# Filler matmuls between the waits of TensorE in a four-network graph kernel

## The reference

```
# GIN, 3 layers                                 # GATv2, 3 layers, 4/4/1 heads
edge_emb = edge_attr @ W + b                    m = xl[src] + xr[dst] + edge_attr @ We
msg  = relu(h_in[src] + edge_emb)               s = sum(leaky(m) * att)          per head
agg  = segment_sum(msg, dst)                    ex = exp(s - segment_max(s)[dst])
z    = two dense layers of (h_in + agg)         out = segment_sum(xl[src] * ex) / segment_sum(ex)
```

## Time and profile before

| | us |
|---|---|
| median of 3 runs | 11196.97 (11195.04 to 11202.61) |
| the profiled execution, own time | 11203.72 |
| its span, first to last instruction | 11201.9 |
| TensorE, busy | 7487.5 |
| VectorE, busy | 5111.4 |
| POOL, busy | 4643.1 |
| ScalarE, busy | 3374.1 |

### The profile page before, as it was taken

How to read it: one execution, slowest core, us unless ns; L and a number is a source line. 1 busy time by engine, 2 the same in 40 slices (tenths; PEclk the granted TensorE clock), 3 DMA queues, 4 the chain that set the end, 5 groups by cost and what they waited for, 6 DMA issues and landing times.

```text
span 11201.9 us, 174392 instructions
## 1 busy us (share of the span) xinstructions
PE 7487.5 (67%) x43333; PEld 4918.1 (44%) x43334; DVE 5111.4 (46%) x14634; ACT 3374.1 (30%) x10389; POOL 4643.1 (41%) x5386
## 2 busy tenths in 40 slices
PE   5999999567765666556665566665656665666665
PEld 2444598344443333333333444444444443444443
DVE  5888731211111111111115556666555666555667
ACT  1001220111120111111114445555444555444444
POOL 0000000566546666466554444443444443444442
PEclk9999999778877778777787777777777777777777
DMA  1001285222221111111112222221222221222221
GB/s 36 18 35 47 118 333 183 63 69 72 69 65 48 49 47 48 44 49 47 46 42 55 58 58 58 58 57 52 59 57 57 58 58 53 59 58 60 58 59 49
DMA packets 501741, 731.50 MB, mean 65 GB/s; under 512 B 128746, under 2 KB 406593, under 8 KB 485012
## 3 DMA queue, kind: packets, MB, share of 16 engines
q1 hardware_dynamic: 350484, 414.14, 11.2%
q0 software_dynamic: 150528, 308.58, 10.5%
HBM read 597.78 MB, written 124.32 MB: 64 GB/s over the span
## 4 chain that ended last, share of the span: by engine, by line
PE 24%; issue 18%; another core or an unknown queue 14%; DVE 13%; DVEq 2%; ACT 0%; DMA 0%; SPq 0%; POOL 0%; ACTq 0%; POOLq 0%
PE ps L806 5%; PE ps L982 4%; PE ps L918 4%; PE ps L910 4%; PE ps L985 3%; DVE ps L1428 2%; PE ps L993 2%; PE ps L1019 1%; DVE hr L1465 1%; DVE w L1417 1%; DVE w L1433 1%; DVE scanned L1423 1%; DVE sval L1410 1%; DVE mdif L1404 1%
## 5 line engine op out<-in xcount | busy, mean ns | idle before, releaser
L543 POOL DMA_INDIRECT rows_and_onehots<-node_table,idx x4704 | 4511.3, 959 | 2494.0 <-issue 1368.2
L806 PE MATMUL ps<-rows_and_onehots,w 128*128 128x128 f32 x5280 | 921.6, 330 | 1374.6 <-issue 1318.5
L538 POOL COPY idx<-src_g 128x8 int32 (+1 forms) x594 | 114.0, 192 | 3902.4 <-DMA node_table<-hr 2327.6
L806 PEld LDWEIGHTS ps<-rows_and_onehots,w 128*128 128x128 f32 x5280 | 830.1, 235 | 1880.7 <-issue 1768.6
L1290 DVE TENSOR_TENSOR agg<-agg,ps 128x128 f32 x660 | 189.5, 287 | 3027.3 <-remote 2036.4
L678 ACT ACTIVATE w<-ps 128x512 f32<-128x512 f32 x663 | 395.8, 597 | 3308.1 <-remote 1983.2
L1019 PE MATMUL ps<-ident,scanned 20*128 20x20 f32 (+1 forms) x1332 | 328.9, 322 | 1352.5 <-DVE scanned L1423 982.2
L1417 DVE TENSOR_TENSOR w<-rows_and_onehots,ps 128x512 f32<-128x512 f32 x669 | 458.7, 686 | 1644.9 <-remote 1451.2
L982 PE MATMUL ps<-w_L_gnn_We,hr 128*128 128x512 f32 x1344 | 1078.6, 896 | 97.8 <-issue 45.1
L985 PEld LDWEIGHTS ps<-xrb,w 128*128 128x128 bf16 x8064 | 704.2, 123 | 606.0 <-issue 606.0
L993 PE MATMUL ps<-hr,rows_and_onehots 128*128 128x132 f32 (+1 forms) x5280 | 920.7, 327 | 2.2 <-DVE hr L1465 2.2
(11 more groups left out here) (227 smaller groups left out, 11269.6 us busy)
## 6 DMA issues: line engine op xcount, KB each, us to landing
w<-turned_onehots_bf SPq DMA_DIRECT2D x672, 128.0 KB
rows_and_onehots<-node_table,idx POOLq DMA_INDIRECT x4704
hr<-in_ea SPq DMA_DIRECT2D x672, 64.0 KB
w<-adjacency_turned SPq DMA_DIRECT2D x26, 1600.0 KB, 7.1
adjacency<-rows_and_onehots SPq DMA_DIRECT2D x25, 1600.0 KB, 5.2
adjacency_turned<-rows_and_onehots SPq DMA_DIRECT2D x25, 1600.0 KB, 13.0
rows_and_onehots<-adjacency_turned SPq DMA_DIRECT2D x24, 1600.0 KB, 7.6
turned_onehots_bf<-w SPq DMA_DIRECT2D x224, 128.0 KB
```

What stands on the lines that cost most here:

```text
L543: pool.indirect_dma_start(out=G[q][:, (i % CH) * D:(i % CH + 1) * D], out_offset=None, in_=table[:, :], in_offset=bass.IndirectOffsetOnAxi ...
L806: m = pe.matmul(bank(u % 2, P), rows[u][:, c * D:(c + 1) * D], OH[u][:, c * P:(c + 1) * P], start=(c == 0), stop=(c == CH - 1))
```

## The change

TensorE gets a helper that issues matmuls whose results nobody reads. Each multiplies the bits of the constant `ones`, read as bf16, with the bits of `iota_s`, read as bf16 (464 columns), into PSUM bank 6. Three of them follow each `scatter` in `gin 0`, eight in `gin 1` and `gin 2`, and three precede each `look_up` in the GAT passes. Nothing else is changed; no semaphore is added, and no engine but TensorE gets another instruction.

```diff
+FILL_GIN_0, FILL_GIN, FILL_GAT = 3, 8, 3
...
+            def keep_busy(n):
+
+                for _ in range(n):
+                    pe.matmul(bank(6, 2 * NSP), ones[:, :].bitcast(BF16)[:, 0:P], iota_s[:, :].bitcast(BF16),
+                              start=True, stop=True)
...
                     scatter(s, u, S).then_inc(S["scattered"], 1)
+                    keep_busy(FILL_GIN_0 if turns else FILL_GIN)
                     add_rows(s + 1, (u + 1) % RING)
...
                     if on(s + 1):
+                        keep_busy(FILL_GAT)
                         look_up(s + 1, (u + 1) % RING)
```

## The result

The changed kernel took 11400.98 us (median of 4 runs, 11369.94 to 11413.86), the kernel before 11199.79 us beside it (11195.04 to 11221.63): ratio **1.0172** (95% interval 1.0147 to 1.0196). The forecast was 11530, +333 us; measured are +201, and 11401 lies inside the forecast's own range, 11300 to 11780. It is slower by well over 0.2%. The profiled execution took 11401.46 us, 197.7 more than the one before.

The account below looks back on a forecast made before the run. Bound: cycles of POOL's run plus the path from late release to freed slots. Terms 20 + 150 + 165 = 335 us on 11203.7, less 6.7, gave about 11530 us; range 11060 to 11780, the forecast's own 11300 to 11780.

Parts of the forecast that it names:

- What bounds the kernel: Gather passes run in cycles: POOL's run plus the path from the late release to the next slots freed.
- gin 1 and gin 2, 150 us forecast: Fillers between scatter and `add_rows` delay POOL after late releases: 75 us a pass, 150 us, ends 0 and 420.
- My 75 us: Cost taken for each of gin 1 and gin 2, between 0 and 210 us, with 75 late releases a pass.
- Rival (c): Fewer steps pass before matmuls are held; gin 1 cycles carry two groups, 94 us a pass lost: 11670 us, chance 0.20.
- but for less long: GIN passes: clock still down after most waits, but for a shorter time, the step after the release being denser.
- Rival (a): Fillers hold the clock up through waits: GIN costs nothing, GAT wins 36 us a pass, 11090 us, chance 0.20.
- gin 0, 20 us forecast: Three fillers between scatter and `add_rows` in gin 0 cost 20 us, ends 0 and 115.
- GAT, 165 us forecast: Three fillers ahead of `look_up` cost 55 us a pass, 165 us in all, ends -108 and +267.
- fillers at the lower clock make this chain 1.0 us longer: GAT chain from late release through `scan_back` to POOL's gather: 1.17 - 0.15 = 1.0 us, 89 us a pass.
- (b): Late releases come earlier, hanging on TensorE's own state; 1 us sooner each gives 515 us: 10680 us, chance 0.10.
- (d): Nothing changes because all fillers lie in waits: 11197 us, chance 0.08.
- What would show it: Signs: later `rectify` with POOL waiting, POOL's idle time up, GAT `seg_rhs` ended by `scan_back`, dense stages before 2000 us unchanged.

Follow-up runs that it names:

- e2_gin_only: Fillers in the GIN passes alone (3, 8, 8 a step), none in the GAT passes, against the kernel before: ratio 1.0198.
- e3_narrow: GIN passes' fillers alone (3, 8, 8 a step), each 16 columns wide instead of 464, against the kernel before: ratio 1.0107.
- e9_two_f32: Two f32 fillers of 464 columns a step in gin 1 and gin 2 alone, replacing eight bf16 ones, against the kernel before: ratio 1.0124.
- e1_gat_only: Fillers in the GAT passes alone (3 a step), none in the GIN passes, against the kernel before: ratio 1.0010.
- e7_gat_narrow9: Nine fillers of 16 columns a step in the GAT passes, none in the GIN passes, against the kernel before: ratio 1.0047.
- e8_before_again: The kernel before, unchanged, profiled again beside the experiments: 11190.39 us.

## Why the prediction was right, and where it was not

**What bounds the kernel.** Right for `gin 1`, where the growth of 91 us is in POOL's waits: for `add_rows` 90 us more, for held effects 28 less, and 32 more put down to nobody. The GAT passes run in such cycles too.

**gin 1 and gin 2, 150 us forecast, 178 measured** (91 and 87), and 225 for the GIN passes with their ends in `e2_gin_only`. The size is near, and the path is the forecast's: `add_rows` behind a late release comes later by the fillers' time, and POOL waits for it. The number of late releases that I took as given was about right: ScalarE's `rectify` had 75 of these waits in the earlier trace rows, and in the changed kernel (window 3344 to 4650)

```profile
ACT w L679 <- remote: 509.3, 65, 27.7
```

The term that was mis-sized is the price of one. My 75 us are 1.0 us for each of 75; measured, the next `rectify` came 5.97 us after one held in a stop, 4.48 before (medians), 1.5 us later. 65 times 1.5 is 97 us, near the 91 and 87. What the sum had no term for is what becomes of POOL's run: it is parted into four and eight gathers. **Rival (c)** had a run of two groups and then a held effect each time, so more held effects. In the changed kernel these are fewer, its runs of eight (13.11 us) mostly follow a stop without a held effect, and that (c)'s 94 us a pass is nearer to the 91 and 87 than my 75 is luck. But (c)'s mechanism is real: it is what `e3_narrow` does, where 77 runs of eight gathers end held. It acts within the wide fillers' loss too, since four records fewer at the same time (`e9_two_f32`) cost 1.24% where eight cost about 1.7% (an estimate from the passes of `e2_gin_only`). As an estimate from `e3_narrow` and `e2_gin_only`, 1.07% and 1.98%, about half of the loss is number and the rest the fillers' time; how the two join in one cycle is not shown.

**The clock in the GIN passes.** I expected it down after most waits "but for less long". It is (0.58 from 3488 to 3495, 1.00 from 3495.5 on, and 0.87 in the pass against 0.78). Rival (a), that the GIN passes cost nothing, fails: with fillers in the wait the clock went to 0.90 and the ratio was that of the narrow ones.

**gin 0, 20 us forecast:** 15 measured.

**GAT, 165 us forecast, -40 in the trace and +0.1% in `e1_gat_only`.** This term failed, at the step "fillers at the lower clock make this chain 1.0 us longer". I had placed the three fillers between the late release and the `scan_back` of the earlier trace rows. They are not there. The changed kernel behind a late release:

```profile
8119.47 0.69 DVE L1426 TENSOR_TENSOR w<-rows_and_onehots,ps 128x512 f32<-128x512 f32 x1 [5.99 <-remote]
...
8120.61 0.61 PE L1028 MATMUL ps<-ident,scanned 20*128 20x20 f32 x2 [3.57 <-issue]
...
8122.43 0.17 DVE L1460 TENSOR_TENSOR maxima_in_parts<-ps,last 128x20 f32<-128x20 f32 x1
...
8123.59 0.68 DVE L1474 TENSOR_TENSOR hr<-rows_and_onehots,ps 128x512 f32<-128x512 f32 x1
...
8124.60 0.19 POOL L539 COPY idx<-src_g 128x8 int32 x1 [5.50 <-DVE hr L1474]
...
8124.91 1.17 PE L814 MATMUL ps<-iota_s,ones 128*128 128x464 bf16 x3
```

VectorE's `add_terms` is released at 8119.47, and `scan_back` (8120.61), the second `seg_rhs` (8122.43), `weigh` (8123.59) and POOL (8124.60) follow; the fillers come at 8124.91. Over `add_terms`' long waits (over 4 us) of `gat 0` to `gat 2` the distances are the same with no filler, three, nine narrow or nine wide: `scan_back` 1.13 us after the release, `weigh` 3.77 (medians; 3.91 in one). Such waits were 199 before, 152 in the changed kernel and 53 with nine wide ones. In the loop's text fillers stand ahead of `scan_back`, but while `add_terms` is held TensorE has already passed them and stands at `scan_back`'s wait for VectorE. Which wait the engine stands in had to be read, and I had read the order of the text. With fillers out of this path, their number costs (`e7_gat_narrow9`), and their columns pay: nine wide ones against nine narrow ones are the distance from 1.0047 to 0.9963, some 94 us, or 31 a pass. Rival (a) had 36 for the clock, and the clock went from 0.74 to 0.90. But the held effects also came more often and were shorter, so that the clock is the cause is the likely reading and not shown. Three fillers just break even.

**Left out of the sum:** the ends of the passes, 36 us, of which 23 after `gin 1` and `gin 2`. The sum had no term for the stretch in which no gather is left.

**Rivals (b) and (d)** fell. In `gin 1` and `gin 2` the held `rectify` came 2.7 us behind the last gather of the run in place of 3.4 (medians), but that goes with shorter runs: behind the few runs of eight before, it was 3.0. And not all fillers lay in waits.

**By "What would show it".** A later `rectify` with POOL waiting for it: yes. POOL's idle time up: yes, in `gin 1` by the 62 us that the two tables of its waits differ (297.0 against 234.9) and more that is put down to nobody. Dense stages unchanged: yes, but for the 7 us put down to chance. `seg_rhs` ended later by `scan_back`: no, the GAT step failed. The Trainium skill's rule on idle gaps (page "TensorE: Matmul & The Clock Gate", section "HAM oscillation — how this bites in real kernels") is borne out on the clock in both kinds of pass (0.74 to 0.90 with nine fillers in GAT, 0.78 to 0.87 in GIN), and the time fell in the GAT passes alone, where the clock is not shown to be the cause.

## What to carry to other kernels

Work that fills an engine's waits is free only where the engine truly stands in the wait when it reaches the work; find that from what it is waiting for in a late cycle, not from the order of the loop. Three things are to be told apart in a filler: its time in the chain that frees the next buffer, its number of instructions, and the clock it wins. The same fillers with few columns give the second nearly alone, and moving them tells of the first. Put them on the passes one by one: here the same idea costs 2% in one kind of pass and, with nine fillers a step, wins 0.4% in the other. And look at the pattern of runs and stops, not only at how many there are: a run of POOL that ends in a held effect and one that ends because the next step is late look alike in a count.

## What the runs showed of the hardware

The effects of TensorE's matmuls were seen by the other engines at once mostly up to some number of them after POOL's restart (most held from 18 to 30 records on in `gin 1` and `gin 2`, by kernel); later ones were seen when POOL's run of gathers was over. Neither a fixed number of matmuls nor a fixed time fits all six kernels. Whether what is counted are the matmuls, their weight loads (one each) or TensorE's instructions of every kind could not be told apart; nor is it shown that the gathers cause it, since no run had other work on POOL. In `gin 0` the edge is less sharp: in `e8_before_again` about a fifth of the effects are held at 8 records already (19 of 94), and 40 of 41 at 22.

A granted clock 0.15 higher over a whole pass (0.75 to 0.90, `gin 1` with narrow and wide fillers in the wait) changed the ratio by 0.0004, although TensorE was busy for 68% of the window or more. The fillers' columns and so their time rose with it, so a higher clock by itself does not tell that a kernel got faster.
